# Phase A of a three-phase transformer kernel: the sine product on GpSimd, token mixing on ScalarE and GpSimd, and a new slot order

## Chip, cores and metric

The kernel runs on one core of one Trainium2 chip. The metric is the device time of one execution in microseconds. Engines are called PE (TensorE), DVE (VectorE), ACT (ScalarE), POOL (GpSimd) and SP (the engine that issues most DMAs).

## What is computed

Input x is 32 sequences of 256 tokens with 128 features. Four blocks follow one another, each of them added to x; phase A of the kernel computes the first two.

```python
# attention (first block), per sequence, 16 heads of 8 features
q, k, v = projections of layernorm(x)
q, k    = rotary(q), rotary(k)       # (xr, xi) -> (xr*cos - xi*sin, xr*sin + xi*cos) * radius(token)
q, k    = layernorm over each head
x       = x + softmax(q k^T / sqrt(8)) v @ out_w + out_b
# ffn (second block), token mixing
xr = mu_r * x + (1 - mu_r) * x_prev  # x_prev: the token before, zero for the first
xk = mu_k * x + (1 - mu_k) * x_prev
x  = x + sigmoid(xr @ W_r^T) * (relu(xk @ W_k^T) ** 2 @ W_v^T)      # on layernorm(x)
```

## The kernel before

The kernel has three phases one after the other. `phase_a` computes attention and ffn for all 32 sequences, `phase_b` and `phase_d` the other two blocks. The change touches `phase_a` alone.

Phase A is a software pipeline. Iteration c works on sequence c in its first stage and on sequences c+1, c-1, ... c-6 in others, so that one iteration issues one sequence's worth of every stage. Each of the five engines runs its own instruction list in order, and semaphores alone tie them. `steps(body)` calls each engine's `body(c)` for c from -2 to 40. On PE, ACT and DVE an iteration is cut into eight slots p = 0 to 7, one for each head pair.

In each slot PE first issues `scores(c-2, p)` (line 244, four matmuls into the one buffer `psS`) and `shifted(c-4, p)` (line 257); DVE answers the first with `row_max` (line 610, a reduction of 1024 columns), ACT the second with `exps` (line 470). The buffer psS is single, so the next slot's scores wait for this slot's row maximum. All the other work is written by hand into slots behind these:

- `proj_q(c)` (lines 297, 298) puts Q and K of sequence c into psA; on DVE `cosine` (636) and `sine` (643) read psA, add a bias and multiply by tables into YC and YS; `centre` on PE (319, 320) rotates and centres both into psA; ACT's `centred` copies and squares it; PE's `var`, DVE's `variance` (650) and eight small steps `rsqrt(c, 0..7)` (657 to 671) make a reciprocal root by Newton's method; ACT's `spread`, PE's `hr_t` and DVE's `normed` (678) follow, then `qk_parts` on ACT (520 to 524) and POOL (813 to 819). SP's `parts` stores the result to memory and `gather` (192, 194) brings it back in another layout for `scores`. Row maxima travel in the same way: `max_t` on PE, `max_parts` on ACT, `max_low` on POOL (823), `max_rows_out` (162) and `max_rows_in` (170) on SP.
- ffn: `fstats` on DVE gives mean and variance (to line 699), `fpower` (827) and `fz` (832, 835) on POOL normalise, `fz_t` on PE (375) transposes into psB, ACT's `fz_t` copies into FZT (534), which has a zero column in front, so that token mixing is done by `ffn_kr` on PE (386, 390) with two matmuls for each product: one with the weights scaled by mu against FZT, one with those scaled by 1-mu against FZT shifted by a column. ACT's `ffn_kr` (539, 541), POOL's `kact` (840), PE's `ffn_v` (397), DVE's `gv` (705) and POOL's `x2` (845) follow.
- `stats` (614 to 627), POOL's `power` (775) and `z` (779, 782), PE's `z_t` prepare sequence c+1. POOL's `x_bias` (788) and `clip` (806, 809) stand beside them. `normalise` (683, 686), `on_t`, `out_proj`, `x1` (693) end attention.

A bank of psum is shared by several of these: the transposes of Z, HX and FZ and the variances all use psB, so PE's `fz_t` waits for DVE's `variance` (semaphore `vareps`).

SP's order in an iteration is `max_rows_out(c-3)`, `load(c+2)`, `max_rows_in(c-3)`, `gather(c-1)`, `parts(c)`, `store(c-6)`; `max_rows_in` waits until the DMA of `max_rows_out` has landed.

## Time and profile before

| | us |
|---|---|
| median of 3 runs | 1571.19 (1564.33 to 1573.87) |
| the profiled execution, its own time | 1572.75 |
| its span, first to last instruction | 1571.0 |
| phase A, to its last GpSimd instruction | about 725 |
| PE busy over the span | 1403.7 |
| DVE / ACT / POOL busy | 1143.7 / 916.6 / 452.0 |

The profile's page gives the busy time of each engine and a picture of the span in 40 slices. Phase A fills the first 18 of them. The timeline lists instructions of an engine in order of time, with equal ones in a row merged (x2, x4), and behind some the idle time before them with what ended it. Spans on POOL and ends of matmuls are rough.

### The profile page before, as it was taken

What the parts mean: (1) busy time and instruction counts of PE and PEld (TensorE: products, weight loads), DVE (VectorE), ACT (ScalarE), POOL (GpSimd) and SP (SyncE); (2) the same over time, 40 slices, a digit from 0 to 9 for tenths busy, and PEclk for the clock granted to TensorE, in tenths of its full rate; (3) what the DMA queues carried; (4) which work ended last, traced back from release to release, by engine and by line L of the source; (5) the groups of instructions that cost most, each with busy time, mean ns of one, the idle gap of its engine ahead of it and who ended that gap; (6) DMA issues with size and microseconds to landing.
All of it is one profiled execution on the core that took longest, in us unless ns stands there. A gap on an engine that the chain in (4) does not pass through costs nothing. (4 is left out here: it accounts for less than half of the span.)

```text
span 1571.0 us, 33090 instructions
## 1 busy us (share of the span) xinstructions
PE 1403.7 (89%) x10741; PEld 915.3 (58%) x10741; DVE 1143.7 (73%) x2899; ACT 916.6 (58%) x2490; POOL 452.0 (29%) x753
## 2 busy tenths in 40 slices
PE   4689999999899899883799999999999998599997
PEld 3345555555555555542566666666666664488886
DVE  5777888888888888722577777777777766287786
ACT  2266777777777777660455555555555553355553
POOL 4335555555455555221000000000100000033322
PEclk7689999999999999996899999999999999799998
DMA  2222222222222222201001000000000000223331
GB/s 71 65 67 63 64 71 73 73 72 74 70 73 73 74 73 71 59 12 54 14 22 31 21 21 26 26 22 21 28 24 22 21 21 21 82 84 85 85 85 38
DMA packets 103123, 80.63 MB, mean 51 GB/s; under 512 B 14423, under 2 KB 95767, under 8 KB 102954
## 3 DMA queue, kind: packets, MB, share of 16 engines
q1 hardware_dynamic: 102106, 78.37, 17.6%
q8 instruction: 89, 1.46, 0.4%
q14 instruction: 80, 0.66, 0.2%
q10 hardware_dynamic: 848, 0.15, 0.1%
HBM read 50.16 MB, written 28.31 MB: 50 GB/s over the span
## 5 line engine op out<-in xcount | busy, mean ns | idle before, releaser
L610 DVE TENSOR_REDUCE a_MX<-a_psS 128x4 f32<-128x1024 f32 x256 | 312.5, 1221 | 78.0 <-PE a_psS L244 78.0
L470 ACT ACTIVATE a_PT<-a_psE 128x512 f32<-128x512 f32 x512 | 278.2, 598 | 77.7 <-PE a_psE L257 74.0
L244 PE MATMUL a_psS<-a_KS,a_QS 48*128 48x256 f16 x1024 | 104.3, 283 | 58.8 <-DVE a_MX L610 37.0
L271 PE MATMUL a_psV<-a_PT,a_VX 128*32 128x256 f32 x2048 | 140.9, 394 | 0.5 <-ACT a_PT L470 0.5
L1422 POOL TENSOR_TENSOR b_SWB<-b_b2col,b_SW 128x128 f32<-128x128 f32 x65 | 26.1, 401 | 317.6 <-ACT b_SW L1172 317.6
L244 PEld LDWEIGHTS a_psS<-a_KS,a_QS 48*128 48x128 bf16 x1024 | 29.9, 95 | 141.6 <-DVE a_MX L610 61.4
L1200 ACT ACTIVATE b_HT<-b_psR 128x512 f32<-128x512 f32 x65 | 38.8, 597 | 124.3 <-PE b_psR L1062 124.3
L257 PE MATMUL a_psE<-a_QS,a_KS 50*128 50x256 bf16 x1024 | 101.2, 275 | 4.6 <-ACT a_PT L470 4.4
L1298 DVE SCALAR_TENSOR_TENSOR b_DZ<-b_U,b_psD 128x512 f32<-128x512 f32 x65 | 44.7, 687 | 81.0 <-PE b_psD L1027 79.4
L1206 ACT ACTIVATE b_PR<-b_psL,b_mx 128x128 f32<-128x128 f32 x260 | 92.3, 365 | 5.9 <-DVE b_mx L1322 5.9
L1426 POOL TENSOR_TENSOR b_rs<-b_rs,b_mhalf 128x2 f32<-128x2 f32 x32 | 22.3, 697 | 224.3 <-DVE b_rs L1340 224.3
L271 PEld LDWEIGHTS a_psV<-a_PT,a_VX 128*32 128x32 f32 x2048 | 54.4, 111 | 55.4 <-issue 30.7
L1553 PE MATMUL d_psH<-d_ZT,d_w1n 128*128 128x256 f32 x256 | 62.4, 388 | 19.5 <-DMA d_ZT<-zT 19.5
L813 POOL TENSOR_TENSOR a_KP<-a_QK,a_KP 128x256 f16<-128x256 f32 x32 | 21.4, 669 | 179.9 <-ACT a_KP L520 179.9
L1190 ACT ACTIVATE b_TH<-b_psZ 128x512 f32<-128x512 f32 x65 | 38.8, 597 | 57.8 <-PE b_psZ L1034 57.8
L1049 PEld LDWEIGHTS b_psL<-b_KT,b_QT 128*128 128x128 f32 x520 | 68.9, 193 | 2.2
L1081 PE MATMUL b_psZ<-b_HT,b_w_t 128*128 128x128 f32 x520 | 68.9, 275 | 0.7 <-ACT b_HT L1200 0.7
L1049 PE MATMUL b_psL<-b_KT,b_QT 128*128 128x128 f32 x520 | 69.3, 277 | 0.0
L1027 PE MATMUL b_psD<-b_w,b_ET 128*128 128x512 f32 x130 | 66.7, 595 | 0.9 <-DVE b_ET L1358 0.9
L1056 PE MATMUL b_g<-b_DZ,b_Z 128*128 128x512 f32 x130 | 66.7, 594 | 0.7 <-DVE b_DZ L1298 0.7
L1067 PE MATMUL b_g<-b_HH,b_ER 128*128 128x512 f32 x130 | 66.5, 594 | 0.0
L1033 PE MATMUL b_psZ<-b_w_t,b_XT 128*128 128x512 f32 x130 | 66.4, 592 | 0.0
(257 smaller groups left out, 3516.8 us busy)
## 6 DMA issues: line engine op xcount, KB each, us to landing
a_KS<-kparts SPq DMA_DIRECT2D x64, 192.0 KB
a_QS<-qparts SPq DMA_DIRECT2D x128, 96.0 KB
qparts<-a_QP SPq DMA_DIRECT2D x64, 96.0 KB, 2.2
a_X<-x_in SPq DMA_DIRECT2D x32, 128.0 KB, 2.7
kparts<-a_KP SPq DMA_DIRECT2D x64, 64.0 KB, 2.1
x<-a_X SPq DMA_DIRECT2D x32, 128.0 KB, 2.1
b_X<-x SPq DMA_DIRECT2D x32, 128.0 KB, 2.3
zT<-b_XT SPq DMA_DIRECT2D x32, 128.0 KB, 1.7
```

The costliest lines, as they stand in the source:

```text
L244: mm = nc.tensor.matmul(psS[:, s, t, :], QS[rows, b % UK, p, t * P:(t + 1) * P], KS[rows, b % UK, p, :], start=True, stop=True)
L257: mm = nc.tensor.matmul(psE[s][:, kt, :], KS[rows, b % UK, p, kt * P:(kt + 1) * P], QS[rows, b % UK, p, :], start=True, stop=True)
L271: mm = nc.tensor.matmul(psV[32 * h:32 * h + 32, 0:T], VX[:, b % UV, kt, at:at + 32], PT[:, gg, kt, h, :], start=(gg == 0 and kt == 0), sto ...
L470: nc.scalar.activation(PT[:, g % 2, :, h + s, :], psE[s][:], ACT.Exp).then_inc(S["exp"], 1)
L610: nc.vector.reduce_max(MX[:, b % 2, :].rearrange("q (s n) -> q s n", s=2)[:, :, 2 * p:2 * p + 2], psS[:], AX.X).then_inc(S["max"], 1)
L1027: nc.tensor.matmul(psD[:], ET[:, i % 2, :], w2[:], start=True, stop=True).then_inc(S["dh_ps"], 1)
L1033: nc.tensor.matmul(psZ[:], XT[:, b % UN, PM + t * P:PM + (t + 1) * P], w1_t[:], start=True, stop=False)
L1049: mm = nc.tensor.matmul(psL[:, 2 * pair + blk, :], QT[:, b % 2, pair, 2 * t + blk, :], KT[:, b % 2, t:t + 3 + blk:2 + blk, :], start=False ...
L1056: nc.tensor.matmul(g1[:], Z[:, b % UN, t, :], DZ[:, t, :], start=(i == 0), stop=(i == TILES - 1), skip_group_check=True).then_inc(S["dw1_p ...
L1067: nc.tensor.matmul(g2[:], ER[:, i % 2, :], HH[:, i % 2, :], start=(i == 0), stop=(i == TILES - 1), skip_group_check=True)\
L1081: mm = nc.tensor.matmul(psPred, w2_t[:, n, :], HT[:, n, :], start=(n == 0), stop=(n == NC - 1), skip_group_check=True)
L1206: e = nc.scalar.activation(PR[:, i % 2, n, :], psL[:, n, :], ACT.Exp, bias=mx[:, i % 2, n:n + 1], accum_out=sm[:, i % 2, n:n + 1])
```

## The change

In `phase_a` alone:

- **Sine.** ACT gets `biased(c)`: two activations of [128, 256] that write psA plus bias into the new tile YB. POOL gets `sine(c)`: one product of [128, 512], YB times the sine table into YS. DVE's `sine` is gone. DVE's `cosine` now also waits for `biased`.
- **Token mixing.** ACT's `fz_t` makes four activations of [128, 256] where it made one: FC holds the transposed values times mu_r and mu_k, FP the same shifted by a column times one minus mu. POOL's `mix` adds FC and FP ([128, 512]) into FX. PE's `ffn_kr` needs one matmul for each product, half as many as before. The weights are no longer prepared on POOL.
- **Order.** PE: `max_t` from slot 1 to 2, `out_t` from 3 to 4, `ffn_kr` from 4 to 5, `pv(.,1)` from 5 to 4, `ffn_v` from 7 to 6, `out_proj` from 6 to 7, `pv(.,2)` from 6 to 7. ACT: `proj_v` from slot 7 to slot 1 of the next iteration, `ot(.,1)` to 1, `max_parts` to 2, `ffn_kr` to 5, `ot(.,0)` to 6. DVE: `fstats` ahead of `stats`; slot 3 now holds `variance` and steps 0, 1, 2; slot 4 holds step 3, `normalise`, steps 4 and 5; `gv` moves from slot 7 to 6, ahead of `x1`. POOL: `sine`, `fpower`, `x_bias`, `fz`, `clip`, `max_low`, `power`, `mix`, `z`, `radius`, `kact`, `x2`, `qk_parts`. SP: `gather(c-1)` stands directly behind `max_rows_out(c-3)`, ahead of `max_rows_in` and the load.

```diff
--- before.py
+++ after.py
@@ -51,7 +51,8 @@
-    wr_t, wk_t, wv_t = sb("wr_t", [P, 2, P]), sb("wk_t", [P, 2, P]), sb("wv_t", [P, P])
+    wr_t, wk_t, wv_t = sb("wr_t", [P, P]), sb("wk_t", [P, P]), sb("wv_t", [P, P])
+    past = sb("past", [P, 2])
...
+    YB = sb("YB", [P, 2 * T])
...
-    FZ, FZT = sb("FZ", [P, NT, P]), sb("FZT", [P, 2, 1 + T])
+    FZ, FC, FP, FX = sb("FZ", [P, NT, P]), sb("FC", [P, 2, T]), sb("FP", [P, 2, T]), sb("FX", [P, 2, T])
...
@@ -204,12 +206,12 @@
         def body(c):
             if on(c - 3):
                 max_rows_out(c - 3)
+            if on(c - 1):
+                gather(c - 1)
+            if on(c - 3):
+                max_rows_in(c - 3)
             if on(c + 2):
                 load_next(c + 2)
-            if on(c - 3):
-                max_rows_in(c - 3)
-            if on(c - 1):
-                gather(c - 1)
             if on(c):
                 parts(c)
@@ -314,8 +316,8 @@
 
         def centre(b):
             wait(pe, "cosed", b, per=2)
-            wait(pe, "sined", b, per=2)
-            wait(pe, "sined", b, per=2)
+            wait(pe, "sined", b)
+            wait(pe, "cosed", b, per=2)
             nc.tensor.matmul(psA[:], centre_w[:, 0, :], YC[:], start=True, stop=False)
             nc.tensor.matmul(psA[:], centre_w[:, 1, :], YS[:], start=False, stop=True).then_inc(S["c_ps"], 1)
 
@@ -370,24 +372,21 @@
         def ffn_kr(b):
-            wait(pe, "fzT", b)
+            wait(pe, "mixed", b)
             if b == 0:
-                pe.wait_ge(S["prep"], 5)
+                pe.wait_ge(S["prep"], 3)
             wait(pe, "square", b + 6)
             if b >= B - 6:
                 wait(pe, "gv", b - 1)
-            for back in range(2):
-                nc.tensor.matmul(psA[:, 0:T], wk_t[:, back, :], FZT[:, b % 2, 1 - back:1 - back + T], start=(back == 0), stop=(back == 1))
-            for t in range(NT):
-                for back in range(2):
-                    at = t * P + 1 - back
-                    mm = nc.tensor.matmul(psA[:, T + t * P:T + (t + 1) * P], FZT[:, b % 2, at:at + P], wr_t[:, back, :], start=(back == 0), stop=(back == 1))
+            nc.tensor.matmul(psA[:, 0:T], wk_t[:], FX[:, 1, :], start=True, stop=True)
+            for t in range(NT):
+                mm = nc.tensor.matmul(psA[:, T + t * P:T + (t + 1) * P], FX[:, 0, t * P:(t + 1) * P], wr_t[:], start=True, stop=True)
             mm.then_inc(S["kr_ps"], 1)
 
         def ffn_v(b):
@@ -411,40 +410,40 @@
                     if on(c - 5):
                         pv(c - 5, 3)
                 if p == 1:
-                    if on(c - 3):
-                        max_t(c - 3)
                     if on(c):
                         centre(c)
                 if p == 2:
+                    if on(c - 3):
+                        max_t(c - 3)
                     if on(c - 4):
                         pv(c - 4, 0)
                 if p == 3:
                     if on(c):
                         var(c)
-                    if on(c - 5):
-                        out_t(c - 5)
                     if on(c - 6):
                         fz_t(c - 6)
                 if p == 4:
+                    if on(c - 5):
+                        out_t(c - 5)
+                    if on(c - 4):
+                        pv(c - 4, 1)
+                if p == 5:
                     if on(c - 6):
                         ffn_kr(c - 6)
-                if p == 5:
-                    if on(c - 4):
-                        pv(c - 4, 1)
                     if on(c - 5):
                         on_t(c - 5)
                     if on(c + 1):
                         z_t(c + 1)
                 if p == 6:
+                    if on(c - 6):
+                        ffn_v(c - 6)
+                    if on(c):
+                        hr_t(c)
+                if p == 7:
+                    if on(c - 5):
+                        out_proj(c - 5)
                     if on(c - 4):
                         pv(c - 4, 2)
-                    if on(c):
-                        hr_t(c)
-                    if on(c - 5):
-                        out_proj(c - 5)
-                if p == 7:
-                    if on(c - 6):
-                        ffn_v(c - 6)
                     if on(c + 1):
                         proj_v(c + 1)
 
@@ -501,6 +500,14 @@
+        def biased(b):
+            wait(act, "q_ps", b)
+            if b == 0:
+                act.wait_ge(S["bcol"], 1)
+            wait(act, "sined", b - 1)
+            for k in range(2):
+                nc.scalar.activation(YB[:, k * T:(k + 1) * T], psA[:, k * T:(k + 1) * T], ACT.Identity, bias=bcol[:, k:k + 1]).then_inc(S["biased"], 1)
+
@@ -529,9 +536,14 @@
             nc.scalar.activation(ONT[:], psC[:, 0:T], ACT.Copy).then_inc(S["onT"], 1)
 
         def fz_t(b):
+            if b == 0:
+                act.wait_ge(S["past"], 1)
+                act.wait_ge(S["zeros"], 1)
             wait(act, "fzT_ps", b)
-            wait(act, "kr_ps", b - 2)
-            nc.scalar.activation(FZT[:, b % 2, 1:1 + T], psB[:, 0:T], ACT.Copy).then_inc(S["fzT"], 1)
+            wait(act, "mixed", b - 1)
+            for i in range(2):
+                nc.scalar.activation(FC[:, i, :], psB[:, 0:T], ACT.Copy, scale=vecs[:, 4 + i:5 + i]).then_inc(S["fzT"], 1)
+                nc.scalar.activation(FP[:, i, 1:T], psB[:, 0:T - 1], ACT.Copy, scale=past[:, i:i + 1]).then_inc(S["fzT"], 1)
 
         def ffn_kr(b):
@@ -545,33 +557,36 @@
                 if on(c - 4):
                     exps(c - 4, p)
                 if p == 0:
+                    if on(c):
+                        biased(c)
+                if p == 1:
+                    if on(c):
+                        proj_v(c)
                     if on(c - 5):
                         ot(c - 5, 1)
-                if p == 1:
+                    if on(c):
+                        centred(c)
+                if p == 2:
                     if on(c - 3):
                         max_parts(c - 3)
-                    if on(c):
-                        centred(c)
                 if p == 3:
                     if on(c - 6):
                         fz_t(c - 6)
-                if p == 4:
+                if p == 5:
                     if on(c - 6):
                         ffn_kr(c - 6)
-                if p == 5:
+                    if on(c + 1):
+                        z_t(c + 1)
+                    if on(c - 5):
+                        on_t(c - 5)
+                    if on(c):
+                        spread(c)
+                if p == 6:
                     if on(c - 4):
                         ot(c - 4, 0)
-                    if on(c + 1):
-                        z_t(c + 1)
-                    if on(c):
-                        spread(c)
-                    if on(c - 5):
-                        on_t(c - 5)
                 if p == 7:
                     if on(c):
                         qk_parts(c)
-                    if on(c + 1):
-                        proj_v(c + 1)
 
         steps(body)
 
@@ -631,17 +647,11 @@
                 prepare()
                 dve.wait_ge(S["bcol"], 1)
             wait(dve, "q_ps", b)
+            wait(dve, "biased", b, per=2)
             wait(dve, "c_ps", b - 1)
             for k in range(2):
                 nc.vector.scalar_tensor_tensor(out=YC[:, k * T:(k + 1) * T], in0=psA[:, k * T:(k + 1) * T], scalar=bcol[:, k:k + 1], in1=cosT[:],
                                                op0=ALU.add, op1=ALU.mult).then_inc(S["cosed"], 1)
-
-        def sine(b):
-            wait(dve, "q_ps", b)
-            wait(dve, "c_ps", b - 1)
-            for k in range(2):
-                nc.vector.scalar_tensor_tensor(out=YS[:, k * T:(k + 1) * T], in0=psA[:, k * T:(k + 1) * T], scalar=bcol[:, k:k + 1], in1=sinT[:],
-                                               op0=ALU.add, op1=ALU.mult).then_inc(S["sined"], 1)
 
         def variance(b):
             wait(dve, "var_ps", b)
@@ -713,44 +723,42 @@
                     if on(c):
                         cosine(c)
                 if p == 1:
+                    if on(c - 6):
+                        fstats(c - 6)
                     if on(c + 1):
                         stats(c + 1)
-                    if on(c - 6):
-                        fstats(c - 6)
                 if p == 3:
                     if on(c):
                         variance(c)
+                        rsqrt(c, 0)
                 if p == 4:
                     if on(c):
-                        rsqrt(c, 2)
                         rsqrt(c, 3)
+                    if on(c - 5):
+                        normalise(c - 5)
+                    if on(c):
+                        rsqrt(c, 4)
                 if p == 5:
                     if on(c):
                         rsqrt(c, 6)
-                if p == 0:
+                if p == 6:
                     if on(c):
-                        sine(c)
+                        normed(c)
+                    if on(c - 6):
+                        gv(c - 6)
                 if p == 3:
                     if on(c):
-                        rsqrt(c, 0)
                         rsqrt(c, 1)
+                        rsqrt(c, 2)
                 if p == 4:
                     if on(c):
-                        rsqrt(c, 4)
                         rsqrt(c, 5)
-                    if on(c - 5):
-                        normalise(c - 5)
                 if p == 5:
                     if on(c):
                         rsqrt(c, 7)
                 if p == 6:
-                    if on(c):
-                        normed(c)
                     if on(c - 5):
                         x1(c - 5)
-                if p == 7:
-                    if on(c - 6):
-                        gv(c - 6)
 
                 if c == 0 and p == 0:
                     out_bias()
@@ -794,12 +802,17 @@
 
         def weights():
             pool.wait_ge(late_in, 16 * len(LATE))
-            for w, col in ((wr_t, 4), (wk_t, 5)):
-                nc.gpsimd.tensor_tensor(w[:, 0, :], w[:, 1, :], vecs[:, col:col + 1].broadcast_to([P, P]), ALU.mult).then_inc(S["wprep"], 1)
             nc.gpsimd.tensor_tensor(wv_t[:], wv_t[:], half[:].broadcast_to([P, P]), ALU.mult).then_inc(S["prep"], 1)
-            pool.wait_ge(S["wprep"], 2)
-            for w in (wr_t, wk_t):
-                nc.gpsimd.tensor_tensor(w[:, 1, :], w[:, 1, :], w[:, 0, :], ALU.subtract).then_inc(S["prep"], 1)
+
+        def mix(b):
+            wait(pool, "fzT", b, per=4)
+            wait(pool, "kr_ps", b - 1)
+            nc.gpsimd.tensor_tensor(FX[:], FC[:], FP[:], ALU.add).then_inc(S["mixed"], 1)
+
+        def sine(b):
+            wait(pool, "biased", b, per=2)
+            wait(pool, "c_ps", b - 1)
+            nc.gpsimd.tensor_tensor(YS[:].rearrange("r (k t) -> r k t", k=2), YB[:].rearrange("r (k t) -> r k t", k=2), sinT[:].unsqueeze(1).broadcast_to([P, 2, T]), ALU.mult).then_inc(S["sined"], 1)
 
         def clip(b):
             wait(pool, "rad", b, per=NT)
@@ -847,26 +860,30 @@
         def body(c):
             if c == 1:
                 weights()
+            if on(c):
+                sine(c)
             if on(c - 6):
                 fpower(c - 6)
             if on(c):
-                clip(c)
+                x_bias(c)
             if on(c - 6):
                 fz(c - 6)
+            if on(c):
+                clip(c)
             if on(c - 3):
                 max_low(c - 3)
             if on(c + 1):
                 power(c + 1)
+            if on(c - 6):
+                mix(c - 6)
+            if on(c + 1):
                 z(c + 1)
+                radius(c + 1)
             if on(c - 6):
                 kact(c - 6)
-            if on(c + 1):
-                radius(c + 1)
+                x2(c - 6)
             if on(c):
-                x_bias(c)
                 qk_parts(c)
-            if on(c - 6):
-                x2(c - 6)
 
         steps(body)
```

## Rows read from the trace of the kernel before

**Rows 1.** Busy us (instructions) in a stretch: PE, PEld, DVE, ACT, POOL; then PEclk.
```profile
117.20:620.80 503.60, 462.77 (x4577) 280.19 (x4578) 425.65 (x975) 370.45 (x852) 264.63 (x424) 0.99 0.26 71
```

**Rows 2.** Timeline, PE: score matmuls of slot 0; start, us, engine, line, idle before.
```profile
117.21 0.39 PE L244 MATMUL a_psS<-a_KS,a_QS 48*128 48x256 f16 x4 [0.45 <-DVE a_MX L610]
...
301.39 0.39 PE L244 MATMUL a_psS<-a_KS,a_QS 48*128 48x256 f16 x4 [1.44 <-DMA a_QS<-qparts]
...
320.69 0.39 PE L244 MATMUL a_psS<-a_KS,a_QS 48*128 48x256 f16 x4 [0.26 <-DVE a_MX L610]
...
620.79 0.40 PE L244 MATMUL a_psS<-a_KS,a_QS 48*128 48x256 f16 x4 [0.26 <-DVE a_MX L610]
```

**Rows 3.** Waits of PE, 150 to 600 us: total, times, longest.
```profile
PE a_psS L244 <- DMA a_QS<-qparts: 16.8, 14, 2.2
```

**Rows 4.** Timeline, SP's queue, one iteration: row maxima out, first gather DMA.
```profile
330.53 0.79 SPq L162 DMA_DIRECT2D maxrows<-a_MP  x2
...
334.37 0.59 SPq L192 DMA_DIRECT2D a_KS<-kparts  x1
```

**Rows 5.** Timeline, VectorE, the iteration from 301.39.
```profile
303.10 0.88 DVE L636 SCALAR_TENSOR_TENSOR a_YC<-a_psA,a_bcol,a_cosT 128x256 f32<-128x256 f32 x2
...
304.68 1.21 DVE L610 TENSOR_REDUCE a_MX<-a_psS 128x4 f32<-128x1024 f32 x1
...
307.63 1.22 DVE L610 TENSOR_REDUCE a_MX<-a_psS 128x4 f32<-128x1024 f32 x1
309.44 1.23 DVE L610 TENSOR_REDUCE a_MX<-a_psS 128x4 f32<-128x1024 f32 x1 [0.59 <-PE a_psS L244]
310.58 0.21 DVE L650 TENSOR_TENSOR a_vr<-a_psB,a_erad 128x64 f32<-128x64 f32 x1
...
311.30 0.22 DVE L661 TENSOR_TENSOR a_hn<-a_hr 128x64 f32<-128x64 f32 x1
311.81 1.23 DVE L610 TENSOR_REDUCE a_MX<-a_psS 128x4 f32<-128x1024 f32 x1 [0.29 <-PE a_psS L244]
...
313.46 0.52 DVE L667 SCALAR_TENSOR_TENSOR a_hr<-a_hm,a_hr 128x64 f32<-128x64 f32 x1
...
314.16 0.35 DVE L683 RECIPROCAL a_RC<-a_psC 128x32 f32<-128x32 f32 x1
...
314.88 1.21 DVE L610 TENSOR_REDUCE a_MX<-a_psS 128x4 f32<-128x1024 f32 x1
```

**Rows 6.** Timeline, PE, the same iteration: ffn_kr and the next score matmuls.
```profile
311.83 1.13 PE L386 MATMUL a_psA<-a_FZT,a_wk_t 128*128 128x256 f32 x4
...
313.78 0.39 PE L244 MATMUL a_psS<-a_KS,a_QS 48*128 48x256 f16 x4
```

**Rows 7.** Timeline, ScalarE, the same iteration.
```profile
311.39 0.38 ACT L534 ACTIVATE a_FZT<-a_psB 128x256 f32<-128x256 f32 x1 [0.75 <-PE a_psB L375]
...
313.88 0.38 ACT L539 ACTIVATE a_KR<-a_psA 128x256 f32<-128x256 f32 x1 [0.81 <-PE a_psA L390]
314.17 0.38 ACT L541 ACTIVATE a_TH<-a_psA 128x256 f32<-128x256 f32 x1
```

**Rows 8.** Timeline, GpSimd, the same iteration.
```profile
307.80 0.71 POOL L827 TENSOR_TENSOR a_fs<-a_fs,a_mhalf 128x2 f32<-128x2 f32 x1 [3.59 <-DVE a_fs L699]
...
311.17 1.31 POOL L775 TENSOR_TENSOR a_s<-a_s,a_expo 128x6 f32<-128x6 f32 x1
...
313.21 0.69 POOL L782 TENSOR_TENSOR a_Z<-a_Z,a_s 128x256 f32<-128x256 f32 x1
...
315.07 0.73 POOL L788 TENSOR_TENSOR a_X<-a_X,a_ebias 128x256 f32<-128x256 f32 x1
```

**Rows 9.** Groups by line: a GpSimd subtraction half as wide; busy us, mean ns.
```profile
L802 POOL TENSOR_TENSOR a_wr_t<-a_wr_t 128x128 f32<-128x128 f32 x1 | 0.5, 452 | 0.0
```

**Rows 10.** One line each: duration ns min/median/max over the stretch.
```profile
L667 DVE SCALAR_TENSOR_TENSOR a_hr<-a_hm,a_hr x23: 225/519/520, 153.3 to 593.7; 128x64 f32<-128x64 f32 x23
...
L626 DVE TENSOR_SCALAR a_s<-a_mv x32: 168/169/379, 3.9 to 606.7; 128x2 f32<-128x2 f32 x32
```

17 lines of the change are left out of this document (9 added, 8 removed).

## The prediction

> **What bounds the kernel now.** I read the busy times by stretch first. Phase A's 25 middle iterations, from 117.2 to 620.8 us, take 503.6 us, and PE is busy in 92% of it, DVE in 85%, ACT in 74%, POOL in 53%, with TensorE's clock at 0.99 [rows 1]. So no engine is full, and the order in which they wait for each other decides. Only phase A is edited; everything behind about 725 us is taken as it is.
>
> Next the starts of slot 0. Two stand at 117.21 and 620.79, 25 iterations apart: (620.79 - 117.21) / 25 = 20.14 us each. But the one from 301.39 to 320.69 takes 19.30, and the next slot 0 there was released by DVE, while the start at 301.39 had waited 1.44 us for the gather of QS [rows 2]. The waits say how common that is: PE waited 16.8 us for it between 150 and 600 us, in 14 waits [rows 3]. That stretch has 450 / 20.14 = 22.3 iterations, so 0.75 us each. An average iteration is 19.30 of compute, 0.75 of gather, and 0.09 of rest, in which I put the short times at a low clock.
>
> Why the gather is late: in SP's queue the row maxima go out at 330.53, and the first gather DMA follows at 334.37 [rows 4]. Between them lie the load of x and `max_rows_in`, which waits for a landing.
>
> Then one iteration on DVE. With slot 0's scores (301.39) as zero: cosine 1.71, slot 1's row maximum 3.29, slot 2's 6.24, slot 3's 8.05, variance 9.19, slot 4's 10.42, slot 5's 13.49 [rows 5], the next slot 0 at 19.30 [rows 2]. From slot 5's maximum to the next slot 0 is thus 5.81. Slot 4, 3.07 long, is the longest of them.
>
> **The gather's wait.** `gather` now follows `max_rows_out` at once. It starts at 330.53 + 0.79 = 331.32 instead of 334.37, so 3.05 us earlier after the same row maxima [rows 4]. `max_low`, for which SP waits, must not become later: it ended when `power` began, at 311.17 or 9.8 [rows 8], and I get 9.6 below. The longest wait was 2.2 us [rows 3], so all of it goes: -0.75 an iteration. `max_rows_in` and the load get behind six gather DMAs, but their data are needed only in the next iteration.
>
> **PE.** `ffn_kr` takes 313.78 - 311.83 = 1.95 us [rows 6]; half of the matmuls go, 0.97 us. PE's own work falls from 0.92 x 20.14 = 18.5 to 17.5. That alone gives nothing where PE then waits for somebody else; the rest asks for whom.
>
> **Slots 0 and 1: sine.** DVE loses two products, 304.68 - 303.10 = 1.58 for four, so 0.79 [rows 5]. In their place DVE waits for `biased`: two ACT operations of 0.38 at a spacing of 0.29 [rows 7], 0.71 with their start, behind Q and K at 1.71. Cosine starts at 2.45, ends its slot at 3.24, and slot 1's maximum stands at 3.24 instead of 3.29. The 0.79 is spent on the wait. POOL's sine is 512 columns wide, which the trace does not show. A product of 256 takes 0.69 [rows 8], a subtraction of 128 takes 0.45 [rows 9]; by their slope 0.69 + 2 x 0.24 = 1.17, at most twice 0.69 = 1.38 and at least 0.69. I take 1.15, as the two rows are the nearest. It ends at 3.6 where DVE's last product ended at 3.3: the centring comes up to 0.3 us later than before, but slot 2's maximum waits for DVE's two moment blocks (6.24 before, 6.2 after), so this costs nothing. Without that cover it costs 0.3.
>
> **Slots 2 and 3.** Slot 2 is bare (1.81), so slot 3's maximum is at 8.0 and `variance` at 8.0 + 1.14 (309.44 to 310.58) = 9.14, as before [rows 5]. One more Newton step of 0.26 enters slot 3 but there was a wait of 0.29 before slot 4's maximum; that stays at 10.1 to 10.4, and I take 10.3.
>
> **Token mixing, the new chain.** PE may transpose FZ only behind `variance`, so ACT's first activation stays where the copy was, at 10.0 [rows 7]. Four at a spacing of 0.29 end at 10.0 + 0.87 + 0.38 = 11.25. POOL before that: `fstats` now comes first of two equal blocks, half of 304.68 + 1.14 to 307.63, so 0.9 earlier, and `fpower` goes from 6.41 to 5.5. From there POOL has no gap: 307.80 to 312.48 is 4.68 [rows 8], plus `x_bias` 0.73, so `power` begins at 9.6 and ends at 10.9. So `mix` starts at 11.3. An addition of 256 takes 0.73 [rows 8], by the same slope 1.2 for 512 (0.73 to 1.46), end 12.5. `z`, which stood behind `power` at once and ended at 12.51 (313.21 + 0.69), now ends at 12.5 + 1.44 = 13.95. PE's `ffn_kr` is reached at about 12.4 and hardly waits.
>
> **Slot 4, the term that decides.** DVE has at 10.3 + 1.14 = 11.45 step 3, `normalise` (0.72: 314.16 to 314.88), step 4, step 5. Undisturbed: 0.26 + 0.73 + 0.26 + 0.26, slot 5's maximum at 12.95. But step 4 (line 667) has a median of 519 ns and a least of 225 [rows 10]: at 313.46 it met POOL's second Z operation and ended at 313.98, 0.08 behind that one's end at 313.90 [rows 5, 8]. So a DVE operation on two tiles of sbuf stands until POOL's has finished. Step 3 at 11.45 meets `mix`, which runs to 12.5: end 12.6. `normalise` reads psum, 13.3. Step 4 now meets the Z multiplication (13.25 to 13.95): end 14.0. Step 5: 14.3. If step 4 slips in ahead, step 5 is caught instead: about 14.0.
>
> The Trainium skill, SBUF — State Buffer, section SBUF: two separate sides, says the same more sharply: VectorE and GpSimd share a port pair as an exclusive lock, and whoever starts first keeps it for the whole instruction. By that the step at 311.30 should have stood until `power` ended at 312.48; its row shows 0.22 us, so for an operation on six columns the trace disagrees [rows 5, 8]. By the rule slot 4 would start 0.5 later still.
>
> **Slots 5 to 7.** From slot 5's maximum the next slot 0 came 5.81 later. Now `x1` stands ahead of slot 7's maximum and waits for `out_proj`, which moved into slot 7, about 0.15 later; 5.95. `gv` in front costs no more. Next slot 0: 14.0 + 5.95 = 19.95 if both locks bite, 18.9 if none does. I take 19.9, plus the rest of 0.09: 20.0.
>
> **Sum.** (20.14 - 20.0) x 25 = 3.5 us gained. Warm-up: the sine chain there is 0.71 + 0.05 + 1.15 against 1.58, 0.3 us in each of three exposed iterations, +1. Drain: four activations and `mix` add 0.87 + 1.2 to each of the two last serial chains, while half of `ffn_kr` at the low clock gives back 1.7; with `out_proj` behind `ffn_v` +1.5. Together -1. The profiled execution took 1572.75 us (span 1571.0), the median is 1571.19; I predict 1570.
>
> **Rivals.**
>
> *A, the forecast: the gather's wait turns into a wait of DVE for POOL.* 1570, its own range 1560 to 1580. For it speaks the median of step 4. Chance 0.40.
>
> *B, the locks don't bite.* If `mix` and Z fall between DVE's steps, or the spacing of POOL's operations lets each through, an iteration is 18.9 + 0.1: 1.14 x 25 = 28 us less, with +2.5 of the ends about 1546. For it: step 4 once took 225 ns, and PE's 17.5 us leave room for it. Against it: POOL has no gap there. Chance 0.30; with one lock of the two it would be about 1558, and I count as B only what gains over 1%.
>
> *C, slower: `x_bias` meets `stats`.* It moves from the end of POOL's round to 6.2, just where DVE's last small operations of `stats` stand (6.05 and 6.15). Line 626 took 169 ns in the median but 379 once [rows 10]. Caught, it stands until 6.9 and slot 2's maximum goes from 6.2 to 6.9; with the later `variance` the whole mixing chain shifts: 19.95 + 0.1 + 0.7 = 20.75, (20.75 - 20.14) x 25 + 2.5 = 18 us, 1590. It decides from 20.04 on for slower at all, from 20.67 for 1%. Chance 0.22.
>
> *D, the gather's wait stays,* because the row maxima come later. It would need `max_low` 2 us or more behind 9.8: 1570 + 12 = 1582. Against it: its chain on POOL starts 0.9 earlier and has only `x_bias` (0.73) more in it. Chance 0.08.
>
> **Chances and range.** B gives faster by over 1% (below 1555.5), 0.30. A, a quarter of C and most of D lie within 1%, 0.50; the rest of C and D above, 0.20. One per cent, 16 us, is about what a measurement of this kernel can tell from no change. Low end near B's 1546, high near C's 1590: 1548 to 1588 leaves out the outer parts of both, some 2 in 10.
>
> **What the profile would show.** PE's wait of L244 for the DMA gone. DVE's step 3 at about 1.1 us and step 4 or 5 at 0.5. GpSimd's two new operations at 1.1 to 1.25. Slot 0 to slot 0 at 20.0, slot 5's maximum at 14.0; at 13.0 B is right. A reduction of slot 2 at 6.9 and a long line 626 or 627 mean C. What would make me wrong: another chain than slot 4's setting the iteration, above all the one through `qk_parts`, which ends on POOL at about 2.5 of the next iteration, just where `sine` wants to start.

## The result and the profile after

The changed kernel takes 1600.32 us (median of 4, 1599.11 to 1600.96) where the kernel before took 1571.12 beside it: 1.019 times as long, with a 95% interval of 1.016 to 1.0221. Forecast were 1570 and a range up to 1588. The profiled execution of the changed kernel has a span of 1597.3 us.

The first view is the timeline of PE in the changed kernel, at the score matmuls that open slot 0 (start, length in us, engine, line; in brackets, where shown, the idle before and who ended it), as [rows 2].

```profile
44.59 0.61 PE L246 MATMUL a_psS<-a_KS,a_QS 48*128 48x256 f16 x4
...
130.94 0.39 PE L246 MATMUL a_psS<-a_KS,a_QS 48*128 48x256 f16 x4
...
316.21 0.39 PE L246 MATMUL a_psS<-a_KS,a_QS 48*128 48x256 f16 x4
...
336.78 0.40 PE L246 MATMUL a_psS<-a_KS,a_QS 48*128 48x256 f16 x4
...
647.87 0.40 PE L246 MATMUL a_psS<-a_KS,a_QS 48*128 48x256 f16 x4
```

25 iterations end at 647.87: (647.87 - 130.94) / 25 = 20.68 us each, against 20.14; the one from 316.21 takes 20.57, against 19.30. So 25 x 0.54 = 13.4 us come from the middle. The start at 130.94 answers to the one at 117.21, so 13.7 are lost ahead of it. What lies behind the last start takes 1597.3 - 647.87 = 949.4, against 1571.0 - 620.79 = 950.2: nothing is lost there. 13.4 + 13.7 - 0.8 = 26.3, the difference of the spans.

Busy time in those 25 iterations, as [rows 1], and PE's waits from 150 to 600 us, as [rows 3]:

```profile
130.90:647.90 517.00, 464.93 (x4428) 259.38 (x4429) 430.21 (x925) 415.05 (x975) 328.80 (x474) 0.99 0.26 69
```

```profile
PE a_psA L321 <- POOL a_YS L815: 17.0, 22, 0.8
PE a_psS L246 <- DVE a_MX L626: 12.0, 22, 0.6
```

PE is busy in 90% (92% before), and ACT's and POOL's work grew from 370 and 265 us to 415 and 329. The wait for the gather is gone, and PE now stands 17.0 / 22 = 0.77 us an iteration for GpSimd's sine. Where the iteration became longer is read on DVE. The timeline of the changed kernel from 316.21, as [rows 5]:

```profile
318.86 0.87 DVE L653 SCALAR_TENSOR_TENSOR a_YC<-a_psA,a_bcol,a_cosT 128x256 f32<-128x256 f32 x2 [0.93 <-ACT a_YB L509]
319.65 1.21 DVE L626 TENSOR_REDUCE a_MX<-a_psS 128x4 f32<-128x1024 f32 x1
...
322.49 0.17 DVE L642 TENSOR_SCALAR a_s<-a_mv 128x2 f32<-128x2 f32 x1
322.57 0.71 DVE L643 TENSOR_SCALAR a_s<-a_mv 128x4 f32<-128x4 f32 x1
323.19 1.21 DVE L626 TENSOR_REDUCE a_MX<-a_psS 128x4 f32<-128x1024 f32 x1
...
327.36 1.22 DVE L626 TENSOR_REDUCE a_MX<-a_psS 128x4 f32<-128x1024 f32 x1 [0.27 <-PE a_psS L246]
328.50 0.21 DVE L675 SCALAR_TENSOR_TENSOR a_hm<-a_hn 128x64 f32<-128x64 f32 x1
...
329.36 0.57 DVE L677 SCALAR_TENSOR_TENSOR a_hr<-a_hm,a_hr 128x64 f32<-128x64 f32 x1
329.96 0.53 DVE L671 TENSOR_TENSOR a_hn<-a_hr 128x64 f32<-128x64 f32 x1
330.42 1.21 DVE L626 TENSOR_REDUCE a_MX<-a_psS 128x4 f32<-128x1024 f32 x1
...
333.73 0.69 DVE L688 TENSOR_TENSOR a_QK<-a_CS,a_psB 128x512 f32<-128x512 f32 x1 [0.28 <-PE a_psB L341]
334.33 0.41 DVE L715 SCALAR_TENSOR_TENSOR a_GV<-a_TH,a_psA 128x256 f32<-128x256 f32 x1
335.08 0.42 DVE L703 TENSOR_TENSOR a_X<-a_psC,a_X 128x256 f32<-128x256 f32 x1 [0.34 <-PE a_psC L366]
335.42 1.21 DVE L626 TENSOR_REDUCE a_MX<-a_psS 128x4 f32<-128x1024 f32 x1
```

and GpSimd's in the same iteration, as [rows 8]:

```profile
322.50 0.74 POOL L796 TENSOR_TENSOR a_X<-a_X,a_ebias 128x256 f32<-128x256 f32 x1
...
328.58 1.27 POOL L810 TENSOR_TENSOR a_FX<-a_FC,a_FP 128x512 f32<-128x512 f32 x1 [1.36 <-ACT a_FP L546]
329.80 0.61 POOL L787 TENSOR_TENSOR a_Z<-a_X,a_mv 128x256 f32<-128x256 f32 x1
```

The starts of the row maxima, as distances from slot 0's scores in us, give a table of both kernels:

| | slot 1 | 2 | 3 | 4 | 5 | 6 | 7 | next slot 0's scores |
|---|---|---|---|---|---|---|---|---|
| before, from 301.39 | 3.29 | 6.24 | 8.05 | 10.42 | 13.49 | 15.29 | 17.94 | 19.30 |
| after | 3.44 | 6.98 | 8.78 | 11.15 | 14.21 | 16.03 | 19.21 | 20.57 |
| added in the slot ahead | 0.15 | 0.59 | -0.01 | 0.00 | -0.01 | 0.02 | 0.53 | 0.00 |

All of the 1.27 us sits in three places: 0.15 is DVE's wait for `biased`; 0.59 is line 643, a four-column operation at the end of `stats` that stands 0.71 us until `x_bias` on GpSimd is over (322.50 + 0.74 = 323.24, it ends at 323.28), which is called the lock below; 0.53 is slot 6, where `x1` now has `gv` ahead of it and waits for `out_proj`. Line 643 is no chance hit. One line's durations over the stretch (ns least/median/most), changed kernel:

```profile
L643 DVE TENSOR_SCALAR a_s<-a_mv x22: 706/712/718, 158.0 to 592.5; 128x4 f32<-128x4 f32 x22
```

It is caught in 22 iterations of 22. The same line (627) of the kernel before has 161/164/164.

**Ahead of the middle.** Stretch from 40 to 120 us, the kernel before and then the changed one, columns as in [rows 1]:

```profile
40.00:120.00 80.00, 62.10 (x454) 30.98 (x453) 61.33 (x123) 39.09 (x91) 31.35 (x51) 0.77 0.24 66
```

```profile
40.00:120.00 80.00, 60.34 (x356) 29.57 (x357) 51.57 (x106) 34.40 (x80) 32.59 (x48) 0.65 0.21 54
```

The first slot 0 comes at 44.59 instead of 39.97, 4.6 us later. GpSimd's sine stands there behind `qk_parts` in its queue (that one's last operation runs to 31.15) and ends at 32.73, where DVE's sine ended at 29.26. The kernel before, then the changed one:

```profile
28.40 0.86 DVE L643 SCALAR_TENSOR_TENSOR a_YS<-a_psA,a_bcol,a_sinT 128x256 f32<-128x256 f32 x2
```

```profile
31.47 1.26 POOL L815 TENSOR_TENSOR a_YS<-a_YB,a_sinT 128x512 f32<-128x512 f32 x1
```

Not all of the 4.6 us is the queue, though. The very first centring ran at the lower clock in this execution. In the run with the late gather (below), whose sine stands in the same place, it did not, and there the first slot 0 comes at 42.70: 0.2 us of that come from an earlier start and about 1.7 from the clock. The changed kernel, then that run:

```profile
14.42 2.03 PE L321 MATMUL a_psA<-a_YC,a_centre_w 128*128 128x512 f32 x2
```

```profile
14.23 1.10 PE L321 MATMUL a_psA<-a_YC,a_centre_w 128*128 128x512 f32 x2
```

The other 9.1 us fall into the next iterations, in which fewer instructions run in the same time and TensorE's granted clock is 0.65 of full speed where it was 0.77. PE waits more (19.7 of the 80 us against 17.9), and what it has then runs more often at 1.2 GHz. A large part of the loss belongs to the sine part of the change: with the sine back on DVE (a run below) the first slot 0 comes at 41.46 and the fifth at 121.96, 9.0 of the 13.7 us earlier. In another pair of runs that differ in the sine alone (the last two on the changed kernel in the table below), the fifth comes 5.2 us earlier.

### The profile page after: what moved, and what is told of

Read it like the earlier page. It is cut to its first block and busy times, and to the rows that moved or that the text cites. A ratio compares the mean times of both kernels' runs of the same rounds, so it can differ in the third digit from the quotient of the medians.

```text
span 1597.3 us, 32865 instructions
## 1 busy us (share of the span) xinstructions
PE 1399.6 (88%) x10486; PEld 890.6 (56%) x10549; DVE 1145.7 (72%) x2836; ACT 973.9 (61%) x2650; POOL 533.0 (33%) x813
## 5 line engine op out<-in xcount | busy, mean ns | idle before, releaser
L1765 POOL TENSOR_TENSOR d_rs<-d_rs,d_mhalf 128x2 f32<-128x2 f32 x32 | 22.3, 696 | 134.7 <-DVE d_rs L1709 134.7
```

## Experiments

Iteration lengths below are those of an ordinary iteration of the profiled execution, before 19.30 and after 20.57. Ratios are to the kernel before on the same chip, with their 95% intervals. The time hangs on two more figures, the mean of the 25 iterations from the fifth slot 0 on and the start of that slot. They are read from PE's timeline in one execution of each kernel:

| us | ordinary | mean of 25 | fifth slot 0 | ratio |
|---|---|---|---|---|
| before | 19.30 | 20.14 | 117.21 | 1 |
| changed | 20.57 | 20.68 | 130.94 | 1.019 |
| early gather alone, in the kernel before | 19.30 | 19.38 | 120.96 | 0.9889 |
| changed, late gather | 20.58 | 20.77 | 129.28 | 1.0182 |
| changed, `x_bias` back | 20.45 | 20.47 | 131.31 | 1.0183 |
| changed, `clip` first | 20.20 | 20.48 | 129.53 | 1.0131 |
| changed, slot 6 (both edits) | 20.57 | 20.68 | 128.85 | 1.0186 |
| changed, slot 6 and `x_bias` back | 20.57 | 20.61 | 131.00 | 1.0196 |
| changed, `out_proj` in slot 6 | 20.17 | 20.50 | 129.63 | 1.012 |
| changed, sine on DVE | 20.44 | 20.69 | 121.96 | 1.0125 |
| changed, mixing on PE | 21.01 | 21.37 | 128.88 | 1.0271 |
| changed, `clip` first and `out_proj` | 20.09 | 20.50 | 128.28 | 1.0136 |
| changed, those two and sine on DVE | 19.45 | 20.25 | 123.12 | 1.0064 |
| early gather and Newton step, in the kernel before | 19.06 | 19.16 | 121.47 | 0.9844 |

Where the mean lies well above the ordinary length in a run on the changed kernel, some iterations are about 1 us longer, and in those looked at one `pv` in slot 4 takes 1.84 to 1.94 us instead of 1.07: TensorE is at its lower clock there.

**The early gather alone** (in the kernel before).

```diff
             if on(c - 3):
                 max_rows_out(c - 3)
+            if on(c - 1):
+                gather(c - 1)
+            if on(c - 3):
+                max_rows_in(c - 3)
             if on(c + 2):
                 load_next(c + 2)
-            if on(c - 3):
-                max_rows_in(c - 3)
-            if on(c - 1):
-                gather(c - 1)
```

> The kernel before with one edit: in SP's order gather(c-1) directly behind max_rows_out(c-3), then max_rows_in, then the load, as in the changed kernel. Theory: the gather's wait is 0.75 us of each middle iteration and all of it goes, mean iteration 20.14 to about 19.4, so 19 us less: ratio 0.988. Rival (the wait would only be replaced, PE then stands for another): ratio 1.00, iterations stay at 20.1 with the wait of L244 put down to DVE.

Ratio 0.9889 (0.9847 to 0.9932). PE has no DMA wait left in the stretch of [rows 3]; its waits there are

```profile
PE a_psS L244 <- DVE a_MX L610: 21.3, 68, 0.5
```

Iterations 19.30, in the mean 19.38 against 20.14. The gather's 0.75 an iteration was real, and nothing else took its place in the middle. Ahead of the middle this execution lost 3.8 us (fifth slot 0 at 120.96, granted clock 0.68 from 40 to 120 us); behind it, it is 3.9 us shorter.

**The early gather taken out of the changed kernel.** SP's order as before.

```diff
                 max_rows_out(c - 3)
+            if on(c + 2):
+                load_next(c + 2)
+            if on(c - 3):
+                max_rows_in(c - 3)
             if on(c - 1):
                 gather(c - 1)
-            if on(c - 3):
-                max_rows_in(c - 3)
-            if on(c + 2):
-                load_next(c + 2)
```

> The changed kernel with SP's old order (load, max_rows_in, then gather). Theory: in the changed kernel the last gather DMA is issued at 14.8 of the iteration; 3.05 us later and 2.75 us to land give 20.6, just at the next slot 0 (20.57): waits of 0 to 0.8 us in some iterations, mean +0.3, ratio 1.024. So the early gather hides little here and its 0.75 us a iteration were mostly covered by the longer iteration. Rival (the early gather earns its full 0.75 here too): ratio 1.031.

1.0182 (1.0149 to 1.0216), mean iteration 20.77 against 20.68. In the changed kernel the order on SP is worth at most 0.1 us, not 0.75 and not the 0.3 expected, and the two ratios can't be told apart. PE has no wait for the gather here either: the iteration is 1.3 us longer than the one of 19.30, and the gather lands within it. The part that alone wins 1.1% is worth next to nothing beside the others.

**The lock at the end of `stats`.** First `x_bias` was put back behind `kact` on GpSimd (in the changed kernel).

```diff
-            if on(c):
-                x_bias(c)
             if on(c - 6):
                 fz(c - 6)
...
                 kact(c - 6)
+            if on(c):
+                x_bias(c)
+            if on(c - 6):
                 x2(c - 6)
```

> The changed kernel with one edit: x_bias(c) back near the end of POOL's round, behind kact, away from the moment where DVE ends stats. Theory (the last operation of stats stands behind x_bias for the shared sbuf port): that operation falls from 0.71 to 0.16 us, slot 1 shortens by 0.55, iteration 20.57 to about 20.0, 25 x 0.55 = 14 us less than the changed kernel, ratio to before about 1.010. Rival (slot 2 is held anyway, because PE waits 0.78 us for GpSimd's sine product): the operation shortens but the iteration stays at 20.4 or more, ratio 1.016 or more.

1.0183 (1.0136 to 1.023), 20.45: almost nothing. Line 643 in that kernel:

```profile
L643 DVE TENSOR_SCALAR a_s<-a_mv x22: 587/588/590, 158.2 to 588.2; 128x4 f32<-128x4 f32 x22
```

`fz` moved up into the gap (in its timeline the subtraction runs 321.76 to 322.39 and line 643 from 321.83 to 322.42). The culprit was not `x_bias` but whatever wide GpSimd operation follows `fpower` there. So in the next one `clip`, two operations on two columns, was put there, with `x_bias` behind it.

```diff
             if on(c):
+                clip(c)
                 x_bias(c)
             if on(c - 6):
                 fz(c - 6)
-            if on(c):
-                clip(c)
```

> The changed kernel with one edit in POOL's order: clip(c) (two operations on two columns) between fpower and x_bias, so that no wide GpSimd operation starts while DVE ends stats. In e2 the last operation of stats still took 588 ns, now behind fz, so e2 did not take the lock away. Theory (the lock makes slot 1 longer by 0.55 us): that operation falls from 0.71 to about 0.17, slot 2's maximum from 6.98 to 6.4, iteration 20.57 to 20.0, mean 20.68 to 20.1, 14 us less than the changed kernel, ratio to before 1.010. Rival (slot 1 and 2 are held by the late sine product anyway): operation short, iteration 20.5, ratio 1.018.

```profile
L643 DVE TENSOR_SCALAR a_s<-a_mv x22: 160/162/165, 156.2 to 586.2; 128x4 f32<-128x4 f32 x22
```

Line 643 is free in all 22, slot 2's maximum is back at 6.44, and an ordinary iteration takes 20.20, 0.37 less. The ratio is 1.0131 (1.0096 to 1.0165), between the theory's 1.010 and the rival's 1.018. Of the 0.54 won at slot 2, 0.16 is lost again before slot 4's maximum (10.77), and 7 of the 25 iterations take about 21.15, so that the mean falls by 0.20 only.

**Slot 6.** Both edits of that slot together, `out_proj` back in slot 6 (PE) and `gv` back in slot 7 (DVE):

```diff
                     if on(c):
                         hr_t(c)
-                if p == 7:
                     if on(c - 5):
                         out_proj(c - 5)
+                if p == 7:
...
-                    if on(c - 6):
-                        gv(c - 6)
...
                         x1(c - 5)
+                if p == 7:
+                    if on(c - 6):
+                        gv(c - 6)
```

> The changed kernel with out_proj back in PE's slot 6 (behind hr_t) and gv back in DVE's slot 7. Theory: slot 6 of DVE, 3.18 us against 2.65 before, is long because x1 waits for out_proj in slot 7 and gv stands ahead of it; it shortens by about 0.5, iteration 20.57 to 20.1, 12 us less than the changed kernel, ratio about 1.011. Rival (slot 6 is held by something that is left as it is, such as the spread and hr_t that come late): iteration stays at 20.5, ratio 1.018.

1.0186 (1.0146 to 1.0225), 20.57: no gain. Slot 6 itself did shorten, from 3.18 to 2.42 us, but slots 1 and 3 and the stretch behind slot 7's maximum grew by 0.33, 0.18 and 0.23. The late `gv` holds up GpSimd, where `x2` stands ahead of `qk_parts` and these ahead of `sine`. Its timelines of GpSimd and PE:

```profile
376.86 0.73 POOL L859 TENSOR_TENSOR a_X<-a_GV,a_X 128x256 f32<-128x256 f32 x1 [4.05 <-DVE a_GV L715]
```

```profile
381.72 1.10 PE L321 MATMUL a_psA<-a_YC,a_centre_w 128*128 128x512 f32 x2 [1.68 <-POOL a_YS L816]
```

PE waits 1.68 us for the sine there, 0.8 in the changed kernel. With `x_bias` back as well (this diff and that of the lock's first run):

> The changed kernel with the edits of e2 and e3 together. Theory: both terms are independent lengths of slots and add: iteration about 19.55, 26 us less than the changed kernel, ratio to before about 1.002. Rival (they hide behind one limit, the chain from qk_parts on POOL into the sine product): no better than the better one of the two, ratio 1.010.

1.0196 (1.0156 to 1.0237), 20.57: neither the theory's 1.002 nor the rival's 1.010, for the same two reasons (line 643 has a median of 588 ns, and `gv` is late). Then `out_proj` alone back in slot 6 (the first half of the diff above), `gv` left ahead of `x1`:

> The changed kernel with out_proj(c-5) back in PE's slot 6 behind hr_t; gv stays in slot 6, so x2 isn't late as it was in e3 (there GpSimd waited 4.05 us for gv and did the sine product 0.9 us later). Theory: x1 no longer waits 0.34 us and slot 6 shortens by 0.4 to 0.5: iteration 20.1, ratio 1.012. But qk_parts and the sine product stay where they are in time, so they come later in the iteration: the centring at about 4.4 to 4.6 after slot 0's scores instead of 4.0. Rival (the chain through exps, qk_parts, sine decides): iteration 20.5, ratio 1.018.

1.012 (1.0077 to 1.0162), 20.17. `x1` no longer waits:

```profile
333.57 0.42 DVE L703 TENSOR_TENSOR a_X<-a_psC,a_X 128x256 f32<-128x256 f32 x1
```

Slot 6 is 2.76 us long, so 0.42 of its 0.53 is `out_proj` behind the wait. The rest stays with `gv` in front, which costs slot 6 more than that rest: without it, in the run with both edits, the slot took 2.42, less than the 2.65 of the kernel before. 8 of the 25 iterations take about 21.1, so the mean falls by 0.18 only.

**Sine and mixing, each undone alone.** The sine back on DVE:

```diff
-            wait(dve, "biased", b, per=2)
...
+        def sine(b):
...
+                nc.vector.scalar_tensor_tensor(out=YS[:, k * T:(k + 1) * T], in0=psA[:, k * T:(k + 1) * T], scalar=bcol[:, k:k + 1], in1=sinT[:],
+                                               op0=ALU.add, op1=ALU.mult).then_inc(S["sined"], 1)
...
                         cosine(c)
+                        sine(c)
...
-            if on(c):
-                sine(c)
```

> The changed kernel with the sine part undone: no biased on ScalarE, both products on DVE in slot 0, the order otherwise as changed. Theory (terms of slot 1: 0.15 from the wait for biased, 0.59 from the lock at the end of stats): only the 0.15 goes, since the lock comes from fpower and x_bias that stay: iteration 20.4, ratio 1.016. Rival (the late sine product, for which PE waits 0.78 us, is the limit): 0.6 us and more, iteration 19.9, ratio 1.008.

1.0125 (1.0088 to 1.0163), 20.44: 0.13 less, as the theory says, with the lock still there (slot 1's maximum at 3.29, slot 2's at 6.84). The ratio is below its 1.016 (though the interval just takes that in), and the middle is not where that comes from: its mean is 20.69, the changed kernel's 20.68. The profiled execution is 8.9 us shorter (span 1588.4 against 1597.3), and the fifth slot 0 comes 9.0 us earlier. So what the sine product on GpSimd costs in time stands in the warm-up. Mixing back on PE with two matmuls a product:

```diff
-            nc.tensor.matmul(psA[:, 0:T], wk_t[:], FX[:, 1, :], start=True, stop=True)
+            for back in range(2):
+                nc.tensor.matmul(psA[:, 0:T], wk_t[:, back, :], FZT[:, b % 2, 1 - back:1 - back + T], start=(back == 0), stop=(back == 1))
...
-            if on(c - 6):
-                mix(c - 6)
```

> The changed kernel with the mixing part undone: one copy on ScalarE, no addition on GpSimd, twelve matmuls' worth on PE, the order otherwise as changed. Theory: DVE's locked steps of slot 4 get free, 0.4 us, but PE is as full as DVE in slot 5 (2.73 us without an idle) and gets 0.97 us more: iteration about 21.1, ratio 1.028. Rival (the four activations and the addition are what makes the changed kernel slow): iteration 20.0, ratio 1.010.

1.0271 (1.0237 to 1.0304), 21.01: 0.44 more. Slot 4 is 0.68 shorter without `mix` beside it, but slots 3 and 5 are 0.46 and 0.53 longer. Of the four parts of the change, mixing on ACT and POOL is thus one that earns in the new layout; the layout around it and the sine cost.

**Clip and slot 6 together** (`clip` ahead of `x_bias`, `out_proj` in slot 6, as above).

> The changed kernel with the edits of e5 and e6, the sine product still on GpSimd. Theory: with the lock gone slot 2's maximum waits for the centring, which the sine product holds until 4.3 (e6): maximum of slot 2 at 6.7, iteration 19.9, so the sine part costs 0.5 us here against the 0.14 that e7 showed; ratio 1.004. Rival (the sine part costs no more than 0.14): iteration 19.55, ratio 0.998.

1.0136 (1.0106 to 1.0166), 20.09: theory (1.004) and rival (0.998) both missed. The two gains don't add: slot 2's maximum stays at 6.73 instead of 6.44, since the chain through `qk_parts` and `sine` now holds the centring. And 10 of the 25 iterations take about 21.1, so the mean is 20.50, no better than with either edit alone. PE's wait for the sine, 17.0 in the changed kernel, is

```profile
PE a_psA L321 <- POOL a_YS L815: 23.9, 22, 1.1
```

**All three undone** (clip first, `out_proj` in slot 6, sine on DVE; mixing as changed).

> The changed kernel with the edits of e5 (clip first), e6 (out_proj in slot 6) and e7 (sine on DVE) together; mixing on ScalarE and GpSimd, the early gather and the rest of the order stay. Theory (the slots add): slot maxima at 3.29, 6.24, 8.05, 10.4, 13.5, 15.3, 18.05 and the next slot 0 at 19.4, so the iteration is back at the stall-free one of the kernel before; ratio 0.992 to 0.996, depending on how often TensorE's clock dips. Rival (a chain not yet seen, e.g. through mixing, holds the iteration): 19.9 or more, ratio above 1.00.

The theory of the chains held: an iteration without a dip takes 19.45, so 1.12 of the 1.27 us are accounted for. The run differs from the last one in the sine alone, which without cover thus costs 0.64 us. The time did not follow: 1.0064 (1.0037 to 1.0091), because nearly every iteration takes 20.4. TensorE's clock dips in them. Stretches of one such iteration (columns as in [rows 1], the clock third from the end):

```profile
315.00:317.00 2.00, 2.00 (x18) 1.16 (x20) 1.35 (x3) 1.81 (x5) 1.21 (x2) 0.69 0.09 20
317.00:319.00 2.00, 2.00 (x22) 0.81 (x16) 1.97 (x5) 0.72 (x2) 1.86 (x3) 0.50 0.60 171
319.00:321.00 2.00, 2.00 (x20) 1.47 (x18) 1.93 (x5) 1.57 (x4) 0.70 (x3) 0.96 0.67 176
```

At 0.50, the lower level of 1.2 GHz, `pv` takes 1.93 us instead of 1.07, and the iteration loses 0.95:

```profile
316.60 1.93 PE L273 MATMUL a_psV<-a_PT,a_VX 128*32 128x256 f32 x16
```

**Early gather and one Newton step earlier** (in the kernel before; the gather's diff as above, and on DVE:)

```diff
                         variance(c)
-                if p == 4:
-                    if on(c):
-                        rsqrt(c, 2)
-                        rsqrt(c, 3)
...
                         rsqrt(c, 1)
+                        rsqrt(c, 2)
                 if p == 4:
+                    if on(c):
+                        rsqrt(c, 3)
+                    if on(c - 5):
+                        normalise(c - 5)
                     if on(c):
                         rsqrt(c, 4)
                         rsqrt(c, 5)
-                    if on(c - 5):
-                        normalise(c - 5)
```

> The kernel before with the early gather (e1) and DVE's steps of slots 3 and 4 in the changed order: step 2 in slot 3, then step 3, normalise, steps 4 and 5. Theory (the lock): without mix on GpSimd, normalise lies over the Z multiplication, step 4 starts at 12.55 when that has ended (12.51), takes 0.23 instead of 0.52, and slot 5's maximum comes at 13.1 instead of 13.5. PE, full in slots 4 to 6, lets through about 0.2 of it: iteration 19.1, ratio 0.985. Rival (no lock; step 4's length is its own): 0.52 stays, slot 5 at 13.25.

0.9844 (0.9817 to 0.9871), 1546.58 us beside 1570.9, iterations of 19.06 where the early gather alone has 19.30: faster than both kernels. From the early gather alone only the iterations tell it apart (means 19.16 and 19.38); the intervals of the two ratios overlap. Slot 5's maximum comes at 12.92, where the theory had 13.1 and the rival 13.25. Its timeline of DVE and, below, of GpSimd:

```profile
305.22 0.35 DVE L683 RECIPROCAL a_RC<-a_psC 128x32 f32<-128x32 f32 x1
305.61 0.42 DVE L686 TENSOR_TENSOR a_ON<-a_psC,a_RC 128x256 f32<-128x256 f32 x1
305.95 0.21 DVE L667 SCALAR_TENSOR_TENSOR a_hr<-a_hm,a_hr 128x64 f32<-128x64 f32 x1
306.20 0.23 DVE L661 TENSOR_TENSOR a_hn<-a_hr 128x64 f32<-128x64 f32 x1
```

```profile
305.36 0.61 POOL L781 TENSOR_TENSOR a_Z<-a_Z,a_s 128x256 f32<-128x256 f32 x1
306.48 0.61 POOL L839 TENSOR_TENSOR a_KA<-a_KR 128x256 f32<-128x256 f32 x1 [0.51 <-ACT a_KR L539]
```

The step that stood 0.52 us behind Z in the median [rows 10] now starts 0.02 before Z ends (305.36 + 0.61 = 305.97), takes 0.21, and the next one is done at 306.43, before GpSimd starts again. `normalise` (lines 683 and 686), which reads psum, keeps its lengths of 0.35 and 0.42 us beside Z and fills the time of the lock. Over the stretch of [rows 10] line 667 has a median of 215 ns.

## Why the prediction was wrong, point by point

Two steps failed. One is slot 2, whose lock the sum left out, together with slot 6: they make the middle 16.9 us longer than forecast (+13.4 measured, -3.5 forecast). The other is the warm-up, 12.7 us (+13.7 measured, +1 forecast). With either of them right, the time would have come out at about 1583 or 1588 and so within the range.

- **The gather's wait, -0.75.** Right as a mechanism and, alone, right in size (0.76 in the early-gather run). Wrong was to book it in full in a kernel whose iteration grows: the late-gather run shows that it is worth at most 0.1 there. The sum's form hid that; the base of 19.30 and the gather are alternatives, of which the longer one counts.
- **PE's 0.97 saved.** Right: from `ffn_kr`'s start to the next matmul it is 0.98 us (329.90 to 330.88 in the changed kernel) instead of 1.95. "That alone gives nothing where PE then waits for somebody else" was too pessimistic: undone alone it costs 0.44.
- **Sine.** ACT's pair takes 0.84 us, not 0.71, GpSimd's product 1.26, not 1.15, and slot 1's maximum comes at 3.44, not 3.24. "This costs nothing" held only while `stats` was behind it. In the run with clip and slot 6 it became the chain that holds slot 2, the one through `qk_parts` of which the prediction had warned, and without cover it costs 0.64, not 0.3. Its largest price lies in the warm-up.
- **Slot 2, "6.2 after", is the step of the iteration that failed.** Rival C's mechanism, at a chance of 0.22, was right in place and size: it gave 6.9, measured is 6.98. Its iteration of 20.75 is near the mean of 20.68, but partly by luck, as slot 4 and the stretch behind slot 5 were wrong in opposite ways; and its 1590 lacks the warm-up. The row that should have decided was on the table: line 626 had 379 ns once [rows 10], which showed that an operation with few columns and one input can be caught too, and the two time tables put `x_bias` at 6.2 and the small operations at 6.05 to 6.2. A stronger row of the kernel before was not looked at. Its step 0, a `tensor_scalar` with one input, ends 0.04 to 0.07 us behind `max_low` in 22 of 23 iterations, 0.43 us long in 21 of them (durations, then the timeline; 310.83 + 0.43 = 311.26 and 310.79 + 0.42 = 311.21):

```profile
L657 DVE TENSOR_SCALAR a_hr<-a_vr x23: 195/435/441, 150.4 to 591.1; 128x64 int32<-128x64 int32 x23
```

```profile
310.83 0.43 DVE L657 TENSOR_SCALAR a_hr<-a_vr 128x64 int32<-128x64 int32 x1
```

```profile
310.79 0.42 POOL L823 TENSOR_TENSOR a_MP<-a_MT,a_MP 32x128 bf16<-32x128 f32 x1
```

  A collision that the forecast's own times produce is not a rival but a term. It also takes more than moving `x_bias` to undo it, which the rival did not see.
- **Mixing chain.** Four activations run at a spacing of 0.36 us and take 0.47 each, not 0.29 and 0.38, and start at 10.73, not at 10.0; `mix` 1.27, not 1.2. It came at 12.37, not 11.3, after GpSimd had stood 1.36 us in front of it. No wait on PE followed: `mix` ended at 329.85, and `ffn_kr` started at 329.90 behind other matmuls. But the four activations hold up `exps`, for which PE's line 259 waits 0.17 us in an iteration (3.5 us between 150 and 600 us).
- **Slot 4, "the term that decides".** Two steps stood for GpSimd, as many as forecast, and a third one, step 7, in slot 5 (0.52). But they are steps 4 and 5, since all of DVE came later, and the slot is 3.06 long, not 3.7: `mix` catches step 4 only at its end. Slot 4 was 3.07 before, so it added nothing. By the prediction's own working both locks end at 14.3, and its sum took the 14.0 of the other case. That slot 5's maximum came at 14.21, near the 14.0 forecast, is two errors that cancel: +0.85 ahead of slot 4, -0.64 in it.
- **"5.95" from slot 5's maximum to the next slot 0** measured 6.36. I gave `x1`'s wait for `out_proj` 0.15 and `gv` nothing; slot 6 came out 0.53 longer, 0.42 of it by `out_proj`.
- **The sum.** 19.95 forecast, 20.57 measured: +0.21 up to slot 5 and +0.41 behind it. For the mean, +0.1 of rest is right. (20.68 - 20.0) x 25 = 17 of the 30 us missed.
- **Warm-up, "+1",** measured +13.7 to the fifth slot 0, of which the run with the sine on DVE takes back 9.0 (3.1 ahead of the first slot 0 and 5.9 behind it), and 5.2 in the other pair. I counted the lengthened chain and left out its place in GpSimd's queue (behind `qk_parts`; the sine ends 3.5 us later than before, part of it by the clock) and the clock: [rows 1] covers the middle only, and what happens at 0.65 to 0.77 was not looked at.
- **Drain.** 1570 comes out only with +2.5 for both ends, as the rivals have it, so +1.5 for the drain. The terms listed add up to more: 2 x 2.07 - 1.7 + 1.5 = 3.9. Measured are -0.8 behind the last start. With this slip and the one in slot 4 mended, the sum would have come to about 1581, still 19 us too low.
- **Rivals B and D.** B fell, since line 643 and three Newton steps stood. D fell, since the gather's wait is gone in the trace; its 12 us are not worked out, 25 x 0.75 is 19.

Not settled is how the 9.1 us between the first slot 0 and the fifth split between longer chains and the lower clock, since the sine's run changes both (0.72 instead of 0.65), nor what makes up the 4.7 to 8.5 of the 13.7 us that the sine does not explain. The early gather alone costs 3.8 us there in the kernel before; taken out of the changed kernel it gives back 1.7. All these are single executions. What sets off the clock's dips is open too.

## What to carry to other kernels

Lay the time tables of VectorE and GpSimd over each other for every moved operation, and take each overlap that the tables give as a term of the sum; put an operation that reads psum beside the wide GpSimd one, as `normalise` beside Z in the fastest kernel here. The removal of a wait for an early chain and a longer iteration pay for the same time, so they don't add: run each part alone before the whole. Cost a moved chain in the warm-up too, by its place in the new engine's queue. And set the mean of many iterations beside an ordinary one before you explain a time: here 0.4 us won in the ordinary iteration was 0.2 in the mean.
